# Self attention in a nine-phase decoder kernel: both layer norms moved from VectorE to ScalarE as scale and shift

## What is computed

```python
def _ln(x, g, b):
    m = jnp.mean(x, -1, keepdims=True)
    v = jnp.var(x, -1, keepdims=True)
    return (x - m) * jax.lax.rsqrt(v + 1e-05) * g + b
...
xn = _ln(x, lnx_g, lnx_b)
yn = _ln(y, lny_g, lny_b)
q = jnp.einsum('bsc,hcd->bhsd', xn, wq)
...
a = jax.nn.softmax(jnp.einsum('bhsd,bhtd->bhst', q, k) * D ** (-0.5), axis=-1)
```

## Time and profile before

| | us |
|---|---|
| median of 3 runs | 3989.52 (3985.66 to 3991.07) |
| the profiled execution, its own time | 3961.34 |
| its span | 3959.3 |
| mean granted TensorE clock, as a share of full speed | 0.925 |

### The profile page before, as it was taken

How to read it: one execution, slowest core, us unless ns; L and a number is a source line. 1 busy time by engine, 2 the same in 40 slices (tenths; PEclk the granted TensorE clock), 3 DMA queues, 4 the chain that set the end, 5 groups by cost and what they waited for, 6 DMA issues and landing times. The chain is left out here.

```text
span 3959.3 us, 104241 instructions
## 1 busy us (share of the span) xinstructions
PE 3444.1 (87%) x41696; PEld 2239.8 (57%) x41696; DVE 2546.9 (64%) x5780; ACT 1967.4 (50%) x3810; POOL 1998.7 (50%) x1726
## 2 busy tenths in 40 slices
PE   7888988988599999886999998868888879999676
PEld 3444444544355555564666666645555557777676
DVE  6878878878477677475556647666666645554365
ACT  5555555554255555442665653335555536664254
POOL 5767667666377777654111115436666621111555
PEclk8999999999799999997999999979999979998598
DMA  3212121211920000000000000000000000000386
GB/s 123 76 71 78 69 80 70 77 72 62 297 65 2 2 2 2 16 1 17 5 5 5 5 3 10 5 6 2 2 2 2 2 11 6 7 6 12 99 266 197
DMA packets 48993, 182.11 MB, mean 46 GB/s; under 512 B 11679, under 2 KB 23074, under 8 KB 39361
## 3 DMA queue, kind: packets, MB, share of 16 engines
q1 hardware_dynamic: 44224, 167.68, 12.7%
q0 software_dynamic: 4352, 8.47, 0.6%
HBM read 167.13 MB, written 43.65 MB: 53 GB/s over the span
## 5 line engine op out<-in xcount | busy, mean ns | idle before, releaser
L494 DVE TENSOR_TENSOR_SCAN XC<-ssm_dA,ssm_db 128x2048 f32<-128x2048 f32 x128 | 565.6, 4419 | 145.0 <-PE ssm_db L349 122.0
L556 POOL TENSOR_TENSOR XC<-XC,XB 128x1536 f32<-128x1536 f32 x128 | 492.9, 3851 | 293.1 <-DVE XC L494 180.5
L363 PE MATMUL ssm_y<-XC,ssm_wt 128*128 128x512 f32 x1024 | 493.3, 626 | 1.6 <-POOL XC L556 1.6
L1130 POOL TENSOR_TENSOR self_pm<-self_pT,self_wt 128x512 f32<-128x512 f32 x256 | 321.9, 1292 | 175.6 <-ACT self_pT L904 175.6
L438 ACT ACTIVATE ssm_dA<-ssm_delta,ssm_nega 128x508 f32<-128x508 f32 x512 | 324.9, 707 | 106.2 <-DVE XC L494 106.2
L363 PEld LDWEIGHTS ssm_y<-XC,ssm_wt 128*128 128x128 f32 x1024 | 196.0, 199 | 228.7 <-issue 219.3
L1136 POOL TENSOR_TENSOR XC<-XC,XB 128x128 f32<-128x128 f32 x128 | 58.7, 459 | 402.3 <-DVE XB L1038 402.3
L2332 POOL TENSOR_TENSOR XC<-XC,gla_wt 128x512 f32<-128x512 f32 x128 | 160.6, 1275 | 157.7 <-ACT XC L2183 157.7
L349 PE MATMUL ssm_db<-XB,ssm_dxT 32*128 32x128 f32 x4096 | 174.6, 299 | 71.9 <-DVE XC L494 70.3
L349 PEld LDWEIGHTS ssm_db<-XB,ssm_dxT 32*128 32x128 f32 x4096 | 145.6, 198 | 136.7 <-DVE XC L494 113.0
L1457 DVE TENSOR_REDUCE narrow_nmax<-narrow_scores 128x4 f32<-128x308 f32 x256 | 105.1, 472 | 156.4 <-PE narrow_scores L1274 156.3
(11 more groups left out here) (430 smaller groups left out, 8690.4 us busy)
## 6 DMA issues: line engine op xcount, KB each, us to landing
XB<-c_rows SPq DMA_DIRECT2D x64, 1024.0 KB, 4.7
experts_we<-in_w_experts SPq DMA_DIRECT2D x72, 579.0 KB, 4.6
sorted<-in_padding SPq DMA_DIRECT2D x1, 33280.0 KB, 112.2
experts_rt<-sorted SPq DMA_DIRECT2D x72, 65.0 KB
ssm_xT<-in_xT SPq DMA_DIRECT2D x16, 256.0 KB, 4.6
self_wt<-in_w_self SPq DMA_DIRECT2D x1, 1412.0 KB, 6.5
mlp_wt<-in_w_mlp SPq DMA_DIRECT2D x1, 1347.0 KB, 5.7
cross_ctx_t<-in_ctx SPq DMA_DIRECT2D x16, 77.0 KB
```

Of the source, the lines that this page charges most:

```text
L363: mm = pe.matmul(yp[half][:, :].rearrange("p (b t) -> p b t", b=GROUP), ident, of_state(states(32, at), k), start=False, stop=(nq == 3 and ...
L494: dve.tensor_tensor_scan(states(0, p).rearrange("p m t -> p (m t)"), dA[:, p % 2, :], db[:, :], 0.0, ALU.mult, ALU.add).then_inc(h_ready, 1)
L556: pool.tensor_tensor(states(32, p).rearrange("p (b k) t -> p b k t", k=4)[:, :, 0:3, :], states(0, p).rearrange("p (b k) t -> p b k t", k= ...
L1130: pool.tensor_tensor(pm[:, n % 2, r, :].rearrange("p (h t) -> p h t", h=4), pT[:, n % 2, r, :].rearrange("p (h t) -> p h t", h=4), bcast(V ...
```

## The change

Both norms of the self phase move from VectorE to ScalarE. The subtract and multiply, (x - mean) * rstd, becomes an activation x * rstd + shift with per-row scale and bias. The shift, -mean * rstd, is made by two new small GpSimd instructions (128x4) behind each inverse deviation, and GpSimd's counter of steps goes from 5 to 9 per group. ScalarE does the norms at the end of its beat, behind the evictions of the late jobs: `x1_norm` at p = 1, `in_norm` at p = 3. VectorE keeps the statistics; ahead of them it gains waits on GpSimd's steps, since the mean is now read by GpSimd. In the cross phase the norms stay on VectorE. Ahead of the loop ScalarE does x1_norm(0), in_norm(0), x1_norm(1) in this order, where VectorE had x1_norm(1) ahead of in_norm(0).

```diff
@@
                     act.wait_ge(s2_mm, n - 1)
                 act.activation(nmT[:, n % 2, :], sb[:, 0:T], ACT.Copy).then_inc(nmT_ready, 1)
 
+            def moved(dst, src, k):
+                for b in range(GROUP):
+                    op = act.activation(dst(b), src(b), ACT.Identity, scale=rstd[:, k, b:b + 1], bias=shift[:, k, b:b + 1])
+                return op
+
+            def x1_norm(g):
+                act.wait_ge(pool_step, g * POOL + 4)
+                moved(lambda b: XC[:, g * GROUP + b, :], lambda b: X[:, g * GROUP + b, :], 0).then_inc(x1_normed, 1)
+
+            def in_norm(g):
+                act.wait_ge(pool_step, (g + 1) * POOL)
+                if g:
+                    act.wait_ge(proj_mm, (g - 1) * NJ + 1)
+                moved(lambda b: xin[:, b, :], lambda b: XC[:, g * GROUP + b, :], 1).then_inc(xin_ready, 1)
+
+            def norms(t):
+                g, p = t // GROUP + 2, t % GROUP
+                if own and g < NG:
+                    if p == 1:
+                        x1_norm(g)
+                    if p == 3:
+                        in_norm(g)
+
+            if own:
+                x1_norm(0)
+                in_norm(0)
+                x1_norm(1)
             for g, n in FRONT:
                 empty(g, n)
             for t in BEATS:
@@
                     turned(t)
                 for g, n in late_jobs(t):
                     empty(g, n)
+                norms(t)
 
         @block.vector
         def _(dve):
@@
                 op.then_inc(by_dve, 1)
 
             def x1_stats(g):
+                if g:
+                    dve.wait_ge(pool_step, (g - 1) * POOL + 4)
+                    dve.sem_inc(mark, 1)
                 row_stats(dve, lambda b: X[:, g * GROUP + b, :], stats[:, 0], mv[:, 0], vec, g * VEC, mark)
-
-            def x1_norm(g):
-                dve.wait_ge(pool_step, g * POOL + 2)
-                normalise(dve, lambda b: XC[:, g * GROUP + b, :], lambda b: X[:, g * GROUP + b, :], mv[:, 0], rstd[:, 0])\
-                    .then_inc(x1_normed, 1)
 
             def in_stats(g):
                 if own:
                     dve.wait_ge(x1_ready, g + 1)
+                    if g:
+                        dve.wait_ge(pool_step, g * POOL)
                     dve.sem_inc(mark, 1)
                     row_stats(dve, lambda b: XC[:, g * GROUP + b, :], stats[:, 1], mv[:, 1], vec, g * VEC + 2 * GROUP, mark)
                 else:
@@
                 dve.wait_ge(pool_step, (g + 1) * POOL)
                 if g:
                     dve.wait_ge(proj_mm, (g - 1) * NJ + 1)
-                k = 1 if own else 0
-                normalise(dve, lambda b: xin[:, b, :], lambda b: XC[:, g * GROUP + b, :], mv[:, k], rstd[:, k])\
+                normalise(dve, lambda b: xin[:, b, :], lambda b: XC[:, g * GROUP + b, :], mv[:, 0], rstd[:, 0])\
                     .then_inc(xin_ready, 1)
-                if not own:
-                    normalise(dve, lambda b: ctx_t[0:TK, g % 2, b, :], lambda b: ctx_t[0:TK, g % 2, b, :],
-                              mv[0:TK, 1], rstd[0:TK, 1]).then_inc(xin_ready, 1)
+                normalise(dve, lambda b: ctx_t[0:TK, g % 2, b, :], lambda b: ctx_t[0:TK, g % 2, b, :],
+                          mv[0:TK, 1], rstd[0:TK, 1]).then_inc(xin_ready, 1)
 
             def norms(t):
                 g, p = t // GROUP + 2, t % GROUP
                 if g < NG:
                     if own and p == 0:
                         x1_stats(g)
-                    if own and p == 1:
-                        x1_norm(g)
                     if p == 2:
                         in_stats(g)
-                    if p == 3:
+                    if not own and p == 3:
                         in_norm(g)
 
             def split(n):
@@
 
             if own:
                 x1_stats(0)
-                x1_norm(0)
             in_stats(0)
             if own:
                 x1_stats(1)
-                x1_norm(1)
-            in_norm(0)
+            else:
+                in_norm(0)
             in_stats(1)
             for g, n in FRONT:
                 empty(g, n)
@@
             pool.wait_ge(loaded, 16)
             pool.wait_ge(power_set, 1)
 
+            def shifts(k, base):
+                pool.wait_ge(pool_step, base)
+                pool.tensor_tensor(shift[:, k], mv[:, k, :, 0], rstd[:, k], ALU.mult).then_inc(pool_step, 1)
+                pool.wait_ge(pool_step, base + 1)
+                pool.sem_inc(mark, 1)
+                pool.tensor_scalar(shift[:, k], shift[:, k], -1.0, None, ALU.mult).then_inc(pool_step, 1)
+
             def x1_inv(g):
                 pool.wait_ge(vec, g * VEC + 2 * GROUP)
                 if g:
                     pool.wait_ge(x1_normed, g)
                 pool.sem_inc(mark, 1)
                 inv_std(pool, power[:, :], mv[:, 0], rstd[:, 0], pool_step, g * POOL)
+                shifts(0, g * POOL + 2)
```

More of the change, by code:

```diff
@@ L612, in wide_attention_phase @@
         power = ph.sb("power", [P, GROUP])
+        shift = ph.sb("shift", [P, 2, GROUP])
         if own:
@@ L657, in wide_attention_phase @@
         VEC = 4 * GROUP
-        POOL = 5 if own else 4
+        POOL = 9 if own else 4
         BEATS = range(-1, N + 5)
@@ L1084, in x1_spread @@
                 pool.tensor_tensor(XC[:, gb, :], XC[:, gb, :], bcast(V("g1r"), 1, GROUP), ALU.mult).then_inc(pool_step, 1)
-                pool.wait_ge(pool_step, g * POOL + 3)
+                pool.wait_ge(pool_step, g * POOL + 5)
                 pool.sem_inc(mark, 1)
@@ L1094, in in_inv @@
                     pool.sem_inc(mark, 1)
-                    inv_std(pool, power[:, :], mv[:, 1], rstd[:, 1], pool_step, g * POOL + 3)
+                    inv_std(pool, power[:, :], mv[:, 1], rstd[:, 1], pool_step, g * POOL + 5)
+                    shifts(1, g * POOL + 7)
                 else:
```

## The result

| | before | after |
|---|---|---|
| median of 4 runs each, timed together | 3989.43 us (3985.66 to 3991.07) | 3951.78 us (3946.57 to 3955.42) |
| ratio, 95% interval | | 0.9913 (0.9900 to 0.9925) |
| the profiled execution, its own time | 3961.34 us | 3950.17 us |
| mean granted TensorE clock | 0.925 | 0.927 |

The change makes the kernel faster by 37.7 us by the medians, by 30 to 40 us by the interval of the ratio. The forecast was 29.5 us, with a range of 14.5 to 47.5.

What follows compares the result with a forecast made beforehand. TensorE sets the pace in the self phase, so its waits can be won, chiefly for VectorE's maxima at p = 3. -37.9 + 8.4 = -29.5 us takes 3989.5 to 3960 us, range 3942 to 3975.

Steps and rivals of the forecast that it cites:

- the likeliest case: The forecast itself: 29.5 us less, 3960 us for the kernel, chance 0.69.
- the offset: The runs' median lay 28 us above the profiled execution, unexplained by its trace; the prediction took the difference as kept.
- (1): VectorE loses both norms: 37.9 us less at p = 3, clock falls included; nothing won at p = 1.
- (2): ScalarE's four in_norm activations at p = 3 take 1.65 us and fit in 2.98 us of idle time: 0.
- (3): ScalarE's x1_norm at p = 1 starts the exponentials 0.6 us late: 8.4 us more, ends 0 and 12.6.
- (4): GpSimd makes the shift, 0.65 us behind each inverse deviation: 0; without cover 18 us.
- (5): GpSimd's spread waits for ScalarE's x1_norm, delaying masks, statistics and maxima of p = 2: 0, with 1.2 us to spare.
- (6): Ahead of the loop, shifts and ScalarE norms are added and VectorE's x1_norm(1) lost: 0, within 2 us either way.
- The rival of clock falls: Falls keep coming at their rate, now behind a wait at p = 1: 11.1 us stay, 3971 us; chance 0.16.
- ScalarE was not slowed: Rival: GpSimd's masks hold ScalarE's tiles to 1.32 us, kernel 54 us slower, 4043; chance 0.07 with other losses.
- The rule that adds and multiplies belong on VectorE: By this rule the norms on VectorE cost next to nothing and the change makes the kernel 8 us slower, 3998.

Runs made afterwards that it cites:

- second profile of before: The kernel before, profiled again with no edit: 3979.55 us, loop of the self phase 602.8 us.
- the VectorE form: Kernel before with both norms on VectorE as four subtracts, then four multiplies, each with an accumulated output: 3949.43 us; timed together 3923.42 us, ratio 0.9892.
- x1_norm earlier: Changed kernel with x1_norm on ScalarE ahead of the turned row instead of behind the q evictions: 3924.44 us, ratio 0.9900; timed again 3944.82 us, ratio 0.9910.

## Why the prediction was right

The time lay 8 us under the forecast and inside the range, and the likeliest case is the one that came. The loop got shorter by 27.0 to 31.6 us, which the forecast of 29.5 meets; that the medians differ by more is another matter (the offset, below).

(1) *VectorE loses both norms, 37.9 us less at p = 3.* p = 3 went from 177.5 to 139.6: 37.9. The stretch is 9.30 us (9.29 by the earlier trace rows), and the falls went with the wait. That the sum agrees to the last tenth is luck: against the second profile of before, with six falls, it is 35.9. The removal of the masks shows the cause (340 ns a tile), and in_norm alone gives 37.4. "Nothing is won" at p = 1 is true of this change but not of the norm: with x1_norm on VectorE a stretch takes 9.89 us, without a norm in its way 9.66 (no masks, the VectorE form, x1_norm earlier). The 0.2 us a stretch, some 3 in the loop, are hidden in the change by ScalarE's norm.

(2) *in_norm on ScalarE, 0.* It took the 1.64 us forecast with 1.4 to spare. The sentence that 1.65 us x 14 = 23 would be owed without cover was about the cover of the v jobs; the doubled norm used up all of ScalarE's idle time and cost 0.4 us in the whole loop. So there was cover for twice the work.

(3) *x1_norm on ScalarE, 8.4 us more.* This term had the right mechanism and was too large: p = 1 grew by 5.4 us. The mis-sized step is 1.65 - 1.03 = 0.6 a stretch. The four take 1.64, but the first begins 0.11 before the eviction ends and the exponentials 0.10 before the norm does, so the delay is 0.41. The lower end of the bounds had this overlap in it, and I took 0.6. Order is what costs, as the earlier x1_norm shows: with it p = 1 is 9.66, less than before the change.

(4) *The shift, 0.* Two instructions, 201 and 243 ns as taken from the ssm phase. The hand-over between them is 0.19 us (2.1 us in 11 waits), where two of 0.1 were counted. Nothing waits for them at p = 3, where in_norm begins right behind the turned row. Not tried alone.

(5) *The spread chain, 0 with 1.2 us to spare.* The maxima were forecast to end at 1302.7 and the k jobs at 1303.9, with the turn put off by 0.6 to 1300.08: 2.6 and 3.8 us behind it. They end 2.7 and 3.9 us behind it (1295.60 and 1296.77 against 1292.86). With 2.6 us more it costs 1.4 a group, so both the chain and its slack are shown.

(6) *Ahead of the loop, 0 within 2 us.* The self phase takes 669.1 us before and 637.1 after, and less the loop that is 61.7 and 61.3.

The rival of clock falls was real. Doubling x1_norm made a wait of 2.24 us at p = 1 and brought seven back, in 13 stretches; at 0.72 us none came. ScalarE was not slowed. The rule that adds and multiplies belong on VectorE (the Trainium skill, ScalarE: Activation LUTs, Rules for kernel authors) would have made the kernel slower by 8 us; the runs decide against it for the form of before. With the two-step form the norms can stay on VectorE at the same time (3923.42 us against 3926.09).
*The offset.* "Which nothing in its trace explains; I take the difference as kept" was the right choice, on weak ground: the 18 us behind the narrow phase were to be seen only in a second profile. The loop accounts for 27.0 to 31.6 of the 30 to 40 us that the ratio allows. The 37.7 of the medians are 6 us more than the larger. In the two profiles that share the short stretch behind the narrow phase (not run together) the time falls from 3961.34 to 3924.34, 37.0 us, of which the loop is 32.3. In two that share the long one it falls from 3979.55 to 3950.17, 29.4 us, of which the loop is 27.0. What the remaining 2 to 5 us are isn't settled; the other phases scatter by as much.

## What to carry to other kernels

Before moving work off an engine, compare its shortest and its median instruction: 333 against 1321 ns told that a neighbour held it, and then either another engine or another form of the same instruction wins the same time. Price a moved instruction by the idle time in front of what is queued behind it, stretch by stretch. The same four activations were free at p = 3, cost 0.6 us at p = 1 (0.4 more than VectorE's norm had), and cost nothing at a place 5.5 us ahead of that. And compare loops, not whole profiles: a phase that the change doesn't touch moved a single execution by 18 us.

## What the runs showed of the hardware

- A tensor_scalar with one step and an accumulated output ran at 342 ns beside GpSimd's multiplies of 1.26 us. The one with two steps and without that output took 1321 ns (333 at its shortest), and 340 with the mask multiplies gone.
- In the loop, from 1070 us on, the granted clock fell to 0.50 for 3.4 us behind one TensorE wait of 2.24 us at p = 1 (7 of 13 stretches with x1_norm doubled), and at p = 3 behind 2.0 us with pieces of 0.28, 0.30, 0.37 and 0.37 of idle time in it (6 or 7 of 13). It never fell behind 0.72 us at p = 1 or 1.4 in pieces at p = 2. But it fell once behind pieces of 0.15, 0.37 and 0.37 in the last p = 0 of three profiles (without the masks, and the VectorE form in both its profiles), whose like the other eleven profiles pass without a fall. With x1_norm alone moved 10 of 13 stretches of p = 3 had one. What decides isn't settled.
- Activations of ScalarE that stood ready one behind the other overlapped by 0.10 to 0.11 us, also between an eviction from PSUM, a norm and an exponential.
- The stretch between the narrow phase and the experts took 118 us in some executions and 136 in others, in both kernels. With the long kind goes a wait of VectorE's experts_best that the profile calls remote, 25 to 28 us in four pieces, in ten profiles of ten. Kernels run together were all of one kind; what sets it isn't settled.
